# Landing scatters four at a time, moving attention scratch, reordering ScalarE's start and adding idle products in a gated attention and mixture-of-experts kernel

## The reference, cut to what matters

```
def gat_layer(x, adj, W, a_self, a_neigh, b):          # 8 heads of 32
    feat = einsum('nf,hfo->hno', x, W)
    e = leaky_relu(self[:, :, None] + neigh[:, None, :], 0.2) + (-1e10) * (1 - adj)
    alpha = softmax(e, axis=-1)
    return elu(concat_heads(alpha @ feat + b))
per_graph = layer1(layer0(ctx))                         # ctx 256x64, then 256x256; 4 graphs
x = x + tanh(g0) * vmap(per_graph)(ctx_512, layernorm(x))   # adj is the normalised x
y = layernorm(x)                                        # 1024 tokens of 256
shared = sum over 2 experts of silu(y g_j) * (y u_j) @ d_j  # width 640
routed = top 2 of 8 experts by sigmoid(y w_router), weights divided by their sum
x = x + tanh(g1) * (routed + shared)
```

## Time and profile before

| | us |
|---|---|
| median of 3 runs | 416.96 (414.7 to 417.91) |
| the profiled execution, its time | 419.25 |
| its span in the profile | 417.5 |
| PE busy in the span | 369.5 |
| DVE, ACT, POOL busy | 252.3, 217.8, 92.0 |

### The profile page before, as it was taken

One profiled execution on the slowest core, in us unless ns is written; L12 is line 12 of the kernel. 1 busy time (PEld: TensorE's weight loads), 2 busy tenths in 40 slices (PEclk: granted clock), 3 DMA queues, 4 the chain that ended last, 5 costly groups with the idle time before them and its releaser, 6 DMA issues.

```text
span 417.5 us, 8098 instructions
## 1 busy us (share of the span) xinstructions
PE 369.5 (89%) x2668; PEld 321.7 (77%) x2669; DVE 252.3 (60%) x831; ACT 217.8 (52%) x512; POOL 92.0 (22%) x102
## 2 busy tenths in 40 slices
PE   5987675785998999999993899999999999999990
PEld 4655454564877888788882789999999999999980
DVE  1898979999977988765740432444544444444430
ACT  4699899987677666402100244545455454554310
POOL 6641600001000100017175000122121212212121
PEclk9999898989999999999998699999999999999996
DMA  6149488615032000003899913232323323232121
GB/s 180 35 184 414 168 285 319 259 68 203 2 112 93 0 2 27 0 3 116 312 418 430 401 34 66 32 46 40 39 40 40 47 36 42 42 40 27 25 25 13
DMA packets 30387, 48.69 MB, mean 117 GB/s; under 512 B 19424, under 2 KB 26640, under 8 KB 27408
## 3 DMA queue, kind: packets, MB, share of 16 engines
q1 hardware_dynamic: 24448, 40.80, 27.9%
q0 software_dynamic: 4464, 6.26, 8.5%
q10 hardware_dynamic: 1440, 1.18, 0.9%
HBM read 39.46 MB, written 8.77 MB: 116 GB/s over the span
## 4 chain that ended last, share of the span: by engine, by line
PE 76%; ACT 8%; DVE 8%; another core or an unknown queue 4%; issue 1%; DMA 1%; POOL 0%; ACTq 0%; POOLq 0%; DVEq 0%
PE ps_c L787 20%; PE ps_o L805 12%; PE ps_c L651 12%; PE ps_n L787 5%; PE ps_pt L658 5%; PE ps_pt L568 5%; PE ps_n L651 4%; ACT weights L889 4%; PE ps_o L583 3%; DVE weights L1076 3%; PE ps_f L557 2%; PE ps_n L658 2%; DVE weights L1092 2%; ACT weights L895 2%
## 5 line engine op out<-in xcount | busy, mean ns | idle before, releaser
L787 PE MATMUL ps_c<-tile_t,weights 128*128 128x128 f32 x736 | 89.5, 275 | 0.0
L787 PEld LDWEIGHTS ps_c<-tile_t,weights 128*128 128x128 f32 x736 | 87.6, 192 | 1.2
L1142 DVE SCALAR_TENSOR_TENSOR gate_silu<-gate_tanh,ps_c 128x256 f32<-128x256 f32 x76 | 31.9, 420 | 80.8 <-ACT gate_tanh L989 41.9
L481 POOL DMA_INDIRECT out<-y_sb,tile_in x23 | 35.7, 1554 | 148.2 <-DVE y_sb L1330 148.2
L889 ACT ACTIVATE weights<-weights 128x256 f32<-128x256 f32 x128 | 63.1, 498 | 0.1
L651 PE MATMUL ps_c<-x_norm_t,weights 128*128 128x256 f32 x240 | 57.5, 387 | 1.3 <-DVE hidden L1145 1.3
L1076 DVE SCALAR_TENSOR_TENSOR weights<-weights 128x256 f32<-128x256 f32 x128 | 54.6, 489 | 5.4 <-ACT weights L876 5.1
L994 ACT ACTIVATE weights<-weights 128x2560 f32 x23 | 53.7, 2337 | 7.4 <-issue 7.4
L568 PE MATMUL ps_pt<-ident,weights 128*128 128x128 f32 x256 | 39.7, 306 | 20.0 <-ACT weights L895 20.0
L805 PE MATMUL ps_o<-weights,hidden 128*128 x230 | 53.6, 380 | 0.6 <-DVE hidden L1145 0.6
L568 PEld LDWEIGHTS ps_pt<-ident,weights 128*128 128x128 f32 x256 | 33.4, 159 | 26.5 <-issue 25.7
(11 more groups left out here) (185 smaller groups left out, 466.4 us busy)
## 6 DMA issues: line engine op xcount, KB each, us to landing
weights<-w_routed SPq DMA_DIRECT2D x8, 1920.0 KB, 22.8
weights<-t_rows SPq DMA_DIRECT2D x14, 1024.0 KB, 5.6
weights<-w_shared SPq DMA_DIRECT2D x1, 3840.0 KB, 17.2
tile_in<-slots SPq DMA_DIRECT2D x92, 32.0 KB
slots<-pad_row SPq DMA_DIRECT2D x1, 1188.0 KB, 11.2
out<-y_sb ACTq DMA_DIRECT2D x4, 256.0 KB
weights<-x SPq DMA_DIRECT2D x2, 256.0 KB, 3.7
x_in<-x SPq DMA_DIRECT2D x2, 256.0 KB, 3.7
```

Of the source, the lines that this page charges most:

```text
L481: pool.indirect_dma_start(out=out, out_offset=bass.IndirectOffsetOnAxis(ap=tile_in[:, slot, ID_COL:ID_COL + 1].bitcast(U32), axis=0), in_= ...
L787: mm = pe.matmul(ps_chunk[c][:, part * cw + i * P:part * cw + (i + 1) * P], ring[r % RING][:, a:a + P], tile_t[:, r % 2, k, :], start=(k = ...
```

## The change

1. POOL's scatters wait for those before them: ahead of graph n's four scatters POOL waits until those of graph n - 1 have landed; ahead of the padding scatters until all rows have; and between the fourth and the fifth padding scatter until the four have.
2. Attention scratch now lies in the space of experts 1 to 5, what lives on after it ("tail") in that of experts 6 and 7. SP loads experts 1 to 5 once the last `max_ready`, `probs_turned` and `o_ready` are there, and experts 6 and 7 behind the three waits of before.
3. The base sums of graphs 2 and 3 stay in `x_in[n]` and are stored from there, with a semaphore of their own.
4. The first loads: `w0_t` and `a_cols` come as one array (`first_cols`) on ACT's queue, and graph 0's context is first on SP's queue, in the place of `a_cols`.
5. ACT's first order: `copy_first_wide(0)` and `copy_nodes(0)` stand before `mask_stats(1)`; `exponent(0)` before `copy_features(0)`; `copy_features(1)` moves behind `exponent(1)`; `mask_stats(2)` and the tanh of the gates move to step 2, `mask_stats(3)` to step 6 (`LAST_MASK_AT`), ahead of `copy_nodes(3)`. DVE's wait for the gates moves from step 2 to step 4.
6. PE: `nodes` stand ahead of `weigh` in their steps, and each of steps 0 to 18 ends with four 128x128 products of zeros into `ps_c` (POOL clears `x_norm_t[0]` for them).

```diff
+IDLE_EACH = 4
+LAST_MASK_AT = nodes_at(layer_of(0, 1))
...
-        LATE = 7
-        scratch_at = [(E - LATE) * W_EXP]
+        FIRST_SCRATCH, FIRST_TAIL = 1, 6
+        scratch_at = {"attention": FIRST_SCRATCH * W_EXP, "tail": FIRST_TAIL * W_EXP}
+        base_sum = [y_sb if n < PAIR else x_in[n] for n in range(B)]
...
-            sp.dma_start(a_sb, a_cols.rearrange("(c p) a -> p c a", p=P)).then_inc(ld_a, 16)
+            load_ctx(0)
...
-            for e in range(E - LATE):
+            for e in range(FIRST_SCRATCH):
...
+            sp.wait_ge(max_ready, ALL_UNITS)
+            sp.wait_ge(probs_turned, ALL_UNITS)
+            sp.wait_ge(o_ready, STREAM)
+            load_experts(FIRST_SCRATCH, FIRST_TAIL)
             sp.wait_ge(x_norm_ready, HV * B)
             sp.wait_ge(y_saved, PAIR)
             sp.wait_ge(st_early_rows, 16 * TOPK * HV * PAIR)
-            for e in range(E - LATE, E):
+            load_experts(FIRST_TAIL, E)
...
+            pool.memset(x_norm_t[0], 0.0).then_inc(zeros_ready, 1)
...
                 pool.sem_inc(pool_passed, 1)
+                if 0 < n <= PAIR:
+                    pool.wait_ge(st_early_rows, 16 * TOPK * HV * n)
+                elif n > PAIR:
+                    pool.wait_ge(st_late_rows, 16 * TOPK * HV * (n - PAIR))
...
+            pool.wait_ge(st_late_rows, 16 * TOPK * HV * (B - PAIR))
             for e in range(E):
+                if e == E // 2:
+                    pool.wait_ge(st_pads, 16 * e)
...
+            def idle_products(count):
+                for _ in range(count):
+                    pe.matmul(ps_c[:, 0, 0:P], x_norm_t[0][:, 0, 0:P], x_norm_t[0][:, 1, 0:P], start=True, stop=True)
...
+                if w in NODES_AT:
+                    nodes(NODES_AT[w])
                 if w > 0:
                     weigh(w - 1)
-                if w in NODES_AT:
-                    nodes(NODES_AT[w])
...
+                if w == 0:
+                    pe.wait_ge(zeros_ready, 1)
+                if w < FIRST_FILL - 1:
+                    idle_products(IDLE_EACH)
...
-            act.dma_start(w0_t_sb, w0_t.rearrange("(k p) n -> p k n", p=P)).then_inc(ld_w0_t, 16)
-            act.dma_start(ctx_sb[0][0:F_IN, :], ctx_t[0]).then_inc(ld_ctx[0], 16)
-            act.wait_ge(ld_gates, 16)
-            act.activation(tanh_gates, gates_sb, ACT.Tanh).then_inc(gates_ready, 1)
+            act.dma_start(first_sb, first_cols).then_inc(ld_first, 16)
...
-            mask_stats(1)
             copy_first_wide(0)
             copy_nodes(0)
+            mask_stats(1)
             copy_first_wide(1)
             copy_nodes(1)
+            exponent(0)
             copy_features(0)
-            exponent(0)
-            copy_features(1)
...
+                if w == 0:
+                    copy_features(1)
...
+                if w == LAST_MASK_AT:
+                    mask_stats(B - 1)
                 if w in NODES_AT:
                     copy_nodes(NODES_AT[w])
-                if w == 0:
+                if w == 2:
                     mask_stats(2)
-                if w == UNITS:
-                    mask_stats(3)
+                    act.wait_ge(ld_gates, 16)
+                    act.activation(tanh_gates, gates_sb, ACT.Tanh).then_inc(gates_ready, 1)
...
-                if n > 0:
-                    dve.wait_ge(st_base, 16 * n)
-                dve.scalar_tensor_tensor(out=y_sb, in0=src, scalar=tanh_gates[:, 1:2], in1=x_in[n],
+                if n == 1:
+                    dve.wait_ge(st_base, 16)
+                dve.scalar_tensor_tensor(out=base_sum[n], in0=src, scalar=tanh_gates[:, 1:2], in1=x_in[n],
```

More of the change, by code:

```diff
@@ L137, in gate_col, with build @@
     return 2 * c0 + i * P - c0, 2 * c0 + cw + i * P - c0
-def build(nc, x, ctx_t, w0, w1, w0_t, w1_t, a_cols, gates, bias_t, w_router, w_routed, w_shared, t_rows, slots, out):
+def build(nc, x, ctx_t, w0, w1, first_cols, w1_t, gates, bias_t, w_router, w_routed, w_shared, t_rows, slots, out):
     with ExitStack() as stack:
@@ L169, in build, with carve @@
         wa_sb = sb("wa_sb", [P, 1 + KC, WA_COLS])
-        LATE = 7
-        scratch_at = [(E - LATE) * W_EXP]
-        def carve(shape, dt=F32):
+        FIRST_SCRATCH, FIRST_TAIL = 1, 6
+        scratch_at = {"attention": FIRST_SCRATCH * W_EXP, "tail": FIRST_TAIL * W_EXP}
+        scratch_end = {"attention": FIRST_TAIL * W_EXP, "tail": E * W_EXP}
+        def carve(shape, until="attention"):
             n = 1
@@ L178, in carve @@
                 n *= s
[L179 to L182, removed]
+            a = scratch_at[until]
+            scratch_at[until] = a + n
+            assert scratch_at[until] <= scratch_end[until]
             v = weights[:, a:a + n]
-            if dt != F32:
-                v = v.bitcast(dt)
             if len(shape) == 3:
@@ L188, in carve @@
             return v
-        x_in = [carve([P, HV, D]) if n < PAIR else sb(f"x_in{n}", [P, HV, D]) for n in range(B)]
+        x_in = [carve([P, HV, D], until="tail") if n < PAIR else sb(f"x_in{n}", [P, HV, D]) for n in range(B)]
+        base_sum = [y_sb if n < PAIR else x_in[n] for n in range(B)]
         spare_in = tile_in.rearrange("p s r -> p (s r)")
@@ L209, in build @@
         neg_max = carve([P, AHEAD, QUAD])
[L210 to L215, removed]
+        sums = carve([P, PAIR, HV * HEADS], until="tail")
+        o_inv = carve([P, HV * HEADS], until="tail")
+        invb = carve([P, QUADS, N], until="tail")
+        bias = carve([P, 3, LAYERS * QUADS], until="tail")
+        stats = [carve([P, HV, 8], until="tail") for c in range(PAIR)]
+        att = carve([P, QUADS, N], until="tail")
         inv_wide = att.rearrange("p a (h f) -> p (a h) f", f=FO)
-        elu = [carve([P, QUADS, N]) for c in range(PAIR)]
-        h0_t = [carve([P, KC, N]) for n in range(PAIR)] + [
+        elu = [carve([P, QUADS, N], until="tail") for c in range(PAIR)]
+        h0_t = [carve([P, KC, N], until="tail") for n in range(PAIR)] + [
             v.rearrange("p (k n) -> p k n", k=KC) for v in (spare_in[:, 2 * HV * D:3 * HV * D], spare_t)]
-        rows = [[carve([P, HV, ROW]) for k in range(TOPK)] for n in range(PAIR)] + late_rows
+        rows = [[carve([P, HV, ROW], until="tail") for k in range(TOPK)] for n in range(PAIR)] + late_rows
         def bias_col(kind, layer, quad):
@@ L370, in load_tile, with load_experts @@
                 sp.dma_start(tile_in[:, slot, D:ROW], src[:, D:ROW]).then_inc(r_ld[slot], 16)
+            def load_experts(first, last):
+                for e in range(first, last):
+                    sp.dma_start(weights[:, e * W_EXP:(e + 1) * W_EXP], w_routed[e]).then_inc(ld_expert[e], 16)
+            sp.wait_ge(max_ready, ALL_UNITS)
+            sp.wait_ge(probs_turned, ALL_UNITS)
+            sp.wait_ge(o_ready, STREAM)
+            load_experts(FIRST_SCRATCH, FIRST_TAIL)
             sp.wait_ge(x_norm_ready, HV * B)
@@ L926, in store_base @@
                 act.wait_ge(y_saved, n + 1)
-                act.dma_start(out[n * N:(n + 1) * N, :].rearrange("(h p) d -> p h d", p=P), y_sb).then_inc(st_base, 16)
-            mask_stats(1)
+                act.dma_start(out[n * N:(n + 1) * N, :].rearrange("(h p) d -> p h d", p=P), base_sum[n]).then_inc(
+                    st_base if n < PAIR else st_late_base, 16)
             copy_first_wide(0)
             copy_nodes(0)
+            mask_stats(1)
             copy_first_wide(1)
             copy_nodes(1)
+            exponent(0)
             copy_features(0)
-            exponent(0)
-            copy_features(1)
             for w in range(ALL_UNITS):
```

28 lines of the change are left out of this document (16 added, 12 removed).

## The result

The changed kernel takes 411.46 us (median of 20 runs, 409.76 to 443.3), the kernel before in the same rounds 416.44 us (20 runs, 412.31 to 418.03). The ratio is 0.9903, with an interval of 0.988 to 0.9927. That is 5.0 us less by the two medians and 4.0 us by the ratio, where 15 were forecast. The time lies inside the predicted range, and the gain is about as large as the 1% that the prediction took for the least that can be told from no change.

A forecast was written before the change was run, and what follows sets the result against it. It took PE's late start on tile 0, behind an idle stretch at 211.10 to 229.7 us, as the bound. 8.8 + 2.9 + 0.5 + 3.0 = 15.2 off the median 416.96 gave 402 us; 8-in-10 range 398.5 to 413.

The forecast's parts named there:

- The hole: Idle stretch at 211.10 to 229.7 us: limiting outstanding scatters to four saves PE's 8.8 us wait and 2.9 of low clock.
- What is late next: Tile 0 behind POOL's scatter groups: turned at 241 against products ready at 243.0, so nothing added, 2 us to spare.
- rival (C): POOL's row of landings becomes the bound, tile 0 at 247.3 or later: 406 us, chance 0.14.
- The start: PE's first wide product: graph 0's context is issued at 0.78 instead of 1.33, 0.5 us earlier.
- Steps 0 to 19: Attention: the new order covers two of DVE's three waits for `weigh`, 3.0 us won, bounds 0 and 4.5.
- the products of zeros: PE in the attention steps: 8.5 us of extra products covered by its waits for ACT, taken as 0, bounds -2 and +8.5.
- Rival (E): In the attention, the products of zeros lengthen as many steps as the order shortens; only 11.7 is won: 405, chance 0.13.
- (B): The idle stretch ahead of tile 0 stays or moves once, needing only a load beside scatters: 413.5 us, chance 0.14.
- (D): Slower: loads beside scatters hold PE's signals in two stretches, 188 to 199 and 207 to 217, each costing 11.7: 425, chance 0.07.
- no wait of L923 for remote: Sign in the changed profile: ACT's L923, at the end of the idle stretch before, no longer waits for something unnamed.
- PE without a gap: Sign in the changed profile: PE has no idle time between the last piece of graph 2 and tile 0.
- clock 1.0 there: Sign in the changed profile: PE's granted clock is 1.0 between the last piece of graph 2 and tile 0.

The follow-up runs named there:

- fours_only: The kernel before with POOL's new waits alone added, all seven experts still loaded late; 423.13 us, ratio 1.0151.
- late_loads: The changed kernel without POOL's new waits and with all seven experts loaded late as before the change; 410.07 us, ratio 0.9895.
- before_idle: The kernel before with four products of zeros at the end of steps 0 to 18 as its only edit; 415.47 us, ratio 0.9975.
- no_waits: The changed kernel with POOL's new waits taken out, experts 1 to 5 still loaded early; 404.85 us, ratio 0.9723.
- before_again: The kernel before, unchanged, profiled a second time in one execution; 416.63 us.

## Why the prediction was wrong

**The hole (8.8 + 2.9 of the sum), the step that failed first.** I took a gap of one profiled execution for what bounds the kernel. It stands in one of two profiles of the kernel before, where it cost 2.4 us, and in none of the three other kernels with all loads late (fours_only, late_loads, before_idle), two of which have sixteen scatters in a row beside them. So "the hole belongs to long loads and many outstanding scatters together" has fallen. Its cause stays open: no run showed it a second time, so none could remove it. Two things narrow it. DVE's L1157 was late too, by some 8 us (225.47, with PE's last product for it through at 217.2 and the bytes of the store that it also waits for moved by 194), while POOL issued a scatter every 1.3 us all the time. And nothing speaks for late instructions: the queues that bring them (q8, q14) moved no packet between 205 and 234 us, so none that ended the waits. What the ordinary execution has instead is tile 0 and the ring fill behind the late loads, 7.6 us. My own rows had this case: tile 0 was turned at 247.32 in the profile with the hole, 4.3 us behind the 243.0 at which I wanted PE ready. I asked what is late next only for the new kernel. Asked of the old one, it gives about 247.9 as the earliest start of tile 0, so that removing the hole alone could not have won more than 254.7 - 247.9 = 6.8 of the 11.7, and with 4.9 us of idle time left ahead of it.

**Nor should the median have been lowered by the whole sum.** The 2.3 us by which the profiled execution lay above the median match the 2.4 that the hole had cost. The sum against the profile, 404.0, stands near no_waits (404.85, profiled 405.95), which is luck: no_waits is another kernel, and what it wins is an earlier start of tile 0 and its first chunk at the full clock, by chance 8.8 + 2.9 again, and no hole. Taking the whole 15.2 off the median counted the hole's 2.4 twice.

**"What is late next" (nothing added), the step that failed in the changed kernel.** In place of nothing stand 5.6 us of idle time ahead of tile 0's first chunk and 1.8 us of slow products in it. Group times of 8.9 beside loads and 6.6 alone came out as 12.2 and 13.5 beside loads and 6.5 to 7.0 alone. The 8.9 was four times the 2.2 us at which sixteen outstanding scatters had been served in a row. That is a rate of a full queue; a queue that is drained four times pays each time the way of its last scatter, here 7.8 and 9.4 us beside loads. The group of graph 2 ended at 220.3 instead of 216, graph 3's at 226.8 instead of 223, the padding at 240.4 instead of 236; tile 0 was turned at 245.5 instead of 241. PE was ready at 240.5, one later than the 239.5 forecast. The comparison of 241 with 243.0 also took for granted that the whole row of scatters moves up by the 3.5 us of start and steps, as PE does; 237.5 is what it meant. Graph 0's first scatter did not move (188.4 against 188.0), since beside the loads POOL began it 2.8 us later than it could without them.

So **rival (C)** came true in its mechanism: POOL's row of landings is the bound. Its price was 4.3 us; the runs say 6.6. I had left out that the wait lowers the clock for the chunk behind it, although showed just that behind the hole. "By then the loads are over", which spoke against it, was wrong for graph 2's group among the four late ones (13.5 where 8.9 were reckoned). The fixed time in the Trainium skill, DMA: Bandwidth & Descriptors, section "Anatomy of one DMA — SWDGE (gpsimd) path", some 2.0 us, agrees with the 2.4 to 2.5 us from issue to landing of the groups without loads, and is far from the 7.8 and 9.4 beside them.

**The start (0.5).** Near, 0.7 us in the trace. The product now waits for `first_cols`, which the text had costed at nothing, and no longer for the context.

**Steps 0 to 19 (3.0) and the products of zeros (0).** The sum of the two, 3.0, was near (98.7 against 102.4 and 103.0 with the start's 0.5 in it), and both terms were wrong. Order and start alone leave step 20 at 103.45, no earlier than before: the gain forecast for them is not there. The products alone, on the kernel before, bring 1.8 us, and with the new order 4.8. They cost nothing, as forecast, and they pay, which was only the bound of -2 in the text. What I missed is that the low stretches lie at more places than the three dips I counted: the clock from 20 to 98 us was 0.93 in that profile and 0.89 in before_again. And the two parts help only together: with the products in both, start and order move step 20 from 101.1 to 98.7, which is 2.4 us; without them, nothing. Which piece of the order does it no run separates. **Rival (E)** has fallen. So have **(B)**, whose 413.5 lies as near the measured time as any, and the slower **(D)**: no hole stands in the changed kernel. The sign "no wait of L923 for remote" came true and says nothing, since the kernel before has none in its second profile; "PE without a gap" and "clock 1.0 there" are the signs that failed (5.6 us, 0.83 from 240 to 250).

**Where the rest went.** In spans of single executions, early loads are worth 9.1 us by themselves, start, order and products with them 2.7 more (405.8 to 403.1), and POOL's waits take back 7.5 of the 11.8. 4.3 are left.

## What to carry to other kernels

Before a gap in one execution is put into a sum, look whether another execution has it, and ask of the old kernel too what would be late if the gap were gone. A limit on outstanding DMAs costs the way of the last one at each wait, not the queue's rate, and beside bulk loads that is several times as long; a wait that protects no data should be tried without. Where TensorE idles a little in every step, or just ahead of a step on the path, filler products in the idle time can keep its clock up.

## What the runs showed of the hardware

- 128x128 products of zeros in each of 19 steps raise TensorE's granted clock: from 40 to 60 us it is 0.76 with none, 0.91 with two and 1.00 with four; medians 408.28, 404.92 and 404.85.
- Four scatters of 128 rows, each group landed before the next, take 6.5 to 7.0 us with no expert load beside them and 12.2 to 14.4 beside loads of 1920 KB; the last of them lands 2.4 us after its issue in the one case and 7.8 to 9.9 in the other.
- POOL's first scatter starts 2.5 to 2.8 us after its last copy when no load is out and 5.0 to 5.6 when expert loads are; why is not shown.
- What a wait costs behind itself does not follow from its length alone. The next 32 products took 3.81 us after a wait of 3.9 us (late_loads) and 5.41 after another of 3.9 (before_idle), 6.67 after 4.5, 5.33 after 5.6, 5.42 after 8.9, 6.72 after 11.3, and 3.73 after none.
- In one execution a signal from PE reached ACT some 11 us late, with DMA at 1.00, and DVE was some 8 us late as well; the DMA share was 1.01 from 205 to 235 us in late_loads and from 205 to 240 in before_again, without that. What it was stays open.
